# Copies from input to output issued later in the front of a routed MLP kernel

## What is computed

```
xn = rms_w * (x * rsqrt(mean(x * x) + 1e-6))
gate = xn @ wg_W + wg_b + (cond @ gg_W + gg_b)
gate_w = softmax(gate);  topk_w, topk_i = top_k(gate_w, 2)
h1 = relu(x @ W1[e] + b1[e])      # 256 -> 512
h2 = relu(h1 @ W2[e] + b2[e])     # 512 -> 512
out_e = h2 @ W3[e] + b3[e]        # 512 -> 256
return x + sum over the two chosen e of weight * out_e
```

## Time and profile before

| what | before |
|---|---|
| median of 3 runs | 495.13 us (492.8 to 496.7) |
| the profiled execution's own time | 491.41 us |
| its span, first to last instruction | 489.7 us |
| PE busy | 436.9 us (89%) |
| DVE, ACT, POOL busy | 312.3, 291.6, 296.7 us |
| moved by DMA | 44.74 MB |
| on SyncE's queue of it (q1) | 26.26 MB |
| mean granted TensorE clock | 0.953 |

### The profile page before, as it was taken

How to read it: one execution, slowest core, us unless ns; L and a number is a source line. 1 busy time by engine, 2 the same in 40 slices (tenths; PEclk the granted TensorE clock), 3 DMA queues, 4 the chain that set the end, 5 groups by cost and what they waited for, 6 DMA issues and landing times.

```text
span 489.7 us, 13456 instructions
## 1 busy us (share of the span) xinstructions
PE 436.9 (89%) x4330; PEld 390.8 (80%) x4331; DVE 312.3 (64%) x553; ACT 291.6 (60%) x607; POOL 296.7 (61%) x446
## 2 busy tenths in 40 slices
PE   7606979999999999999999999999999999997860
PEld 6406868998888888888988988898899998887850
DVE  4899755756657756756666567555554545867750
ACT  6607725678678678778776764454455455455540
POOL 4420384567777878677777677856655666473331
PEclk9955699999999999999999999999999999999995
DMA  8929234453454543331334322431222233241011
GB/s 297 394 88 368 98 102 168 120 152 58 125 134 127 141 65 111 55 60 27 62 56 126 56 46 40 63 53 35 54 54 43 43 45 53 34 59 22 2 11 12
DMA packets 18771, 44.74 MB, mean 91 GB/s; under 512 B 3964, under 2 KB 13246, under 8 KB 16542
## 3 DMA queue, kind: packets, MB, share of 16 engines
q0 software_dynamic: 13632, 17.71, 22.0%
q1 hardware_dynamic: 5008, 26.26, 14.5%
q10 hardware_dynamic: 77, 0.04, 0.0%
HBM read 35.60 MB, written 13.50 MB: 100 GB/s over the span
## 4 chain that ended last, share of the span: by engine, by line
PE 40%; POOL 19%; issue 13%; DVE 9%; ACT 8%; DMA 4%; POOLq 2%; DVEq 1%; ACTq 0%
PE bank L1156 27%; PE bank L1197 7%; POOL out L556 6%; PE bank L1134 3%; ACT area L705 3%; DMA out<-area,cto 3%; DVE area L958 3%; POOL area L535 2%; POOL bound L480 2%; DVE area L956 2%; ACT w_hi L659 2%; ACT area L715 1%; DVE stage L982 1%; PE bank L1115 1%; POOL cto L530 1%
## 5 line engine op out<-in xcount | busy, mean ns | idle before, releaser
L1156 PE MATMUL bank<-area,w_hi 128*128 128x256 f16 x1536 | 253.7, 273 | 3.4 <-DVE area L958 3.0
L1156 PE MATMUL bank<-area,w_lo 128*128 128x256 f16 x768 | 209.3, 273 | 0.0
L705 ACT ACTIVATE area<-bank,cprm 128x256 f32<-128x256 f32 (+1 forms) x264 | 132.6, 557 | 71.7 <-PE bank L1156 60.8
L1156 PEld LDWEIGHTS bank<-area,w_hi 128*128 x1536 | 149.7, 98 | 22.3 <-issue 5.2
L956 DVE CAST area<-area 128x512 f16<-128x512 f32 (+1 forms) x144 | 65.0, 451 | 133.5 <-ACT area L705 119.9
L556 POOL DMA_INDIRECT out<-area,cto x71 | 117.3, 1652 | 50.4 <-issue 26.1
L958 DVE TENSOR_TENSOR area<-area 128x512 f16<-128x512 f32 (+1 forms) x144 | 99.1, 688 | 5.0
L535 POOL DMA_INDIRECT area<-in_x,cfrom x65 | 68.9, 1061 | 38.9 <-POOL cfrom L530 27.9
L1197 PE MATMUL bank<-w_hi,area 128*128 x512 | 89.1, 273 | 0.9 <-DVE area L958 0.9
L1156 PEld LDWEIGHTS bank<-area,w_lo 128*128 x768 | 75.1, 98 | 8.7
L715 ACT ACTIVATE area<-area,cw 128x256 f32<-128x256 f32 x71 | 32.2, 501 | 76.1 <-DVE area L963 57.4
(11 more groups left out here) (200 smaller groups left out, 478.1 us busy)
## 6 DMA issues: line engine op xcount, KB each, us to landing
stage<-in_weights SPq DMA_DIRECT2D x10, 1024.0 KB, 6.1
area<-in_x SPq DMA_DIRECT2D x8, 512.0 KB, 7.5
out<-in_x SPq DMA_DIRECT2D x8, 512.0 KB, 12.9
w_lo<-in_weights SPq DMA_DIRECT2D x4, 1024.0 KB
w_hi<-in_weights SPq DMA_DIRECT2D x2, 1024.0 KB, 9.0
out<-area,cto POOLq DMA_INDIRECT x71
area<-in_x,cfrom POOLq DMA_INDIRECT x65
prm<-in_b SPq DMA_DIRECT2D x8, 128.0 KB, 11.8
```

What stands on the lines that cost most here:

```text
L705: ins = act.activation(to[:, m * T + u * wide:m * T + (u + 1) * wide], ps_h[layer][b][:, a * T + u * wide:a * T + (u + 1) * wide], ACT.Rel ...
L1156: ins = nc.tensor.matmul(banks[m // 2][:, (m % 2) * T + u * wide:(m % 2) * T + (u + 1) * wide], weight, xp[:, cols], start=(k == 0 and n = ...
```

## The change

The loop that issues the eight copies is taken from its place behind the loads of x. It now stands in the loop over the experts, and runs once, for the third expert (`FRONT` is 2), behind its two chunks of weights and its row of `b3`. Nothing else differs: the same transfers, sizes and semaphores, and POOL's wait on line 599 as it was.

```diff
@@ -388,9 +388,6 @@
                 sp.dma_start(area[:, c * js * H:(c + 1) * js * H],
                              x.rearrange("(p j) h -> p (j h)", p=P)[:, c * js * H:(c + 1) * js * H])\
                   .then_inc(s_x[c], 16)
-            for n in range(OUT_PARTS):
-                rows = slice(n * N // OUT_PARTS, (n + 1) * N // OUT_PARTS)
-                sp.dma_start(out[rows, :], x[rows, :]).then_inc(s_out0, 16)
             sp.wait_ge(s_order, 1)
             labels = []
 
@@ -412,6 +409,9 @@
                     b3_rows(early)
                 if e >= FRONT:
                     b3_rows(e)
+                for n in range(OUT_PARTS if e == FRONT else 0):
+                    rows = slice(n * N // OUT_PARTS, (n + 1) * N // OUT_PARTS)
+                    sp.dma_start(out[rows, :], x[rows, :]).then_inc(s_out0, 16)
 
 
         @block.gpsimd
```

## The result

| | before | after |
|---|---|---|
| median | 495.33 us (490.85 to 498.54, 20 runs) | 498.26 us (494.74 to 501.57, 20 runs) |
| ratio to before, 95% interval | | 1.0068 (1.0042 to 1.0094) |
| profiled execution, its own time | 491.41 us | 498.44 us |
| span | 489.7 us | 496.7 us |
| mean granted clock | 0.953 | 0.948 |

The time lies in the range of the forecast, but "no change" does not hold: the kernel is slower by about 3 us. Single executions of the two kernels overlap, but the interval leaves out 1; the forecast had taken anything within 1% for something that can't be told from no change, and with 20 executions of each kernel 0.7% can be. Each ratio in this document is the recorded one, over executions in the fast state alone and of the same session, and can differ by up to 0.3% from the plain quotient of the medians (1.0059 here).

A forecast was written before the change was run, and what follows sets the result against it. PE's own work was taken to bound 75 to 415 us, and POOL's chain to the gathers the release of tile 0. Five terms of 0 left the median of 495.1 us at 495 us, range 491.5 to 500.

The forecast's parts named there:

- Taking the copies from 13.5 to 25 us: Front, beside x's loads: removing the copies there gains 0, at most the 1.1 us that ACT once waited for x.
- Issuing: SyncE's queue: the eight issues move behind the third expert's b3 and delay nothing, with 26 us of cover; cost 0.
- Moving the bytes: DMA engines from 52.4 us: the copies take 11.3 us, to 63.7 us, filling an 11.0 us hole; cost 0.
- The gathers: Tile 0's gathers at about 63.4 us: 0.3 us overlap with the copies' tail, cost 0; slow end +2.5 us.
- PE's gap above 4 us: Sign of being wrong: PE's idle gap at 63.4 us ahead of tile 0, expected at 2.8 us, exceeds 4 us.
- a low clock between 60 and 100 us: Sign of being wrong: PE's clock is low in that stretch, where full clock was expected behind the gap.
- the second wait of POOL: Sign of being wrong: POOL's wait behind the maximum over partitions, expected at 9.4 to 9.6 us, exceeds 10.5 us.
- The two long waits of POOL: POOL's 9.57 and 9.42 us waits around the maximum over partitions: +0.15 us at most, counted 0; far end +11.3 us.
- The estimate that was made from the Trainium skill's figure: From approximately 6 us for a fresh GpSimd routine's first call: POOL's second long wait would grow by 1.2 us.
- POOL's wait for the copies: Line 599, ending before the copy at 72.52 us: copies through at 63.7 us leave 8.8 us; cost 0.
- The slower rival: PE's gap at 63.4 us: copies delay tile 0 and PE's clock falls, 506 us or 515 us; chance 0.13.

The follow-up runs named there:

- no_copies: The kernel before without the eight copies and without POOL's wait for them, leaving x out of the output: 493.0 us, ratio 0.9983.
- behind_second: The changed kernel with the copies one expert earlier, behind the second expert's weights: 496.06 us, ratio 1.0072.
- warm_after: The changed kernel with 200 in place of 96 unread matmuls of PE ahead of tile 0: 495.01 us, ratio 1.0039.
- small_packets: The changed kernel with each copy written as 128 pieces of 4 KB in place of 16 of 32 KB; profiled packets stayed 32 KB: 497.0 us, ratio 1.0067.
- pad_after: The changed kernel with 40 one-column memsets added to POOL's program where POOL stands idle: 494.47 us, ratio 0.9993.
- six_late: The changed kernel with two of the eight copies back behind the loads of x and six behind the third expert's weights: 493.9 us, ratio 1.0004.
- extra_pad: The changed kernel with 40 memsets added to POOL's program and four more 512 KB copies queued behind its eight: 499.9 us, ratio 1.0129.
- warm_before: The kernel before with 136 in place of 96 unread matmuls of PE ahead of tile 0: 492.18 us, ratio 0.9984.

## Why the prediction was wrong, by its own steps

*Taking the copies from 13.5 to 25 us* was counted at 0 and was 0: no_copies gives 0.9983, with 1 in its interval, so the kernel before had nothing measurable to gain there.

*Issuing* was right. SyncE's queue issues the copies right behind the third b3, and chunk 6 still goes out only when the gather of tile 1 has landed:

```profile
40.33 5.08 SPq L414 DMA_DIRECT2D out<-in_x  x8
75.68 0.87 SPq L405 DMA_DIRECT2D stage<-in_weights  x2
```

*Moving the bytes* was right in place and order: the copies run from the end of the weights. They take 12.8 us and not 11.3 us, inside the 11.3 to 13.6 us that the forecast allowed; it had read their length off slices that count a packet where it starts, and in the kernel before, too, they take 13.1 us from the first start (13.43 us) to the last end (26.48 us). What failed is the conclusion that they "fill a hole". In that hole the engines carried 24 KB of instructions, 8 KB of them in the row at 58 us on which the chain came to depend. The forecast read the 5 and 2 GB/s of the earlier trace rows as emptiness. A sum of small bytes is not a small dependence.

*The gathers* were counted at 0, with the right question (do they meet the copies' tail) and the wrong transfer. Their data was not late. The step that failed is this one together with the list that it belongs to: it names the gathers as the only transfers that could meet the copies, and **has no term for the fetch of POOL's own instructions**. Measured, that term is 2.9 us of wait in the profile of the changed kernel, and 1.5 to 2.4 us more than the usual 0.57 us in those of behind_second, warm_after and small_packets. The forecast gave the second gather a slack of 2.4 us, and in pad_after the gathers did meet the copies' tail and landed on time. The fetch has only 1 us. Two of the forecast's own signs of being wrong came, PE's gap above 4 us (7.2) and a low clock between 60 and 100 us; the second wait of POOL, at 9.1 us, did not.

*The two long waits of POOL* were counted at 0, which stands: together they are 18.99 us before, 19.63 after, 18.6 in pad_after with the copies beside the second, and 19.0 in no_copies. Their sum varies by up to 2.7 us from profile to profile for a reason that these runs don't give. The estimate that was made from the Trainium skill's figure (GPSIMD Engine Reference, section Instruction dispatch) can't be told from that.

*POOL's wait for the copies* cost nothing, as said: it is behind the gathers, at about 76 us, when the copies had been through for 10 us.

*The slower rival* had the right place, PE's gap, and the right second half: with the longer gap came the low clock. It had three things wrong. The first is the cause of the delay. The second is the point from which it decides, a gap of 4.4 us: the clock fell at or right behind gaps of 2.0 to 4.2 us in seven of the profiles. The third is the price: 18 us at half speed, taken from the one stretch of the front in which the clock had come back only at its end. It came back after 6.8 us here, so that the clock's part is about 1.4 us and not 9. With 2.9 + 1.4 = 4.3 us by the profile of the changed kernel, and 2.2 + 1.4 = 3.6 us with the mean wait of the four profiles named above, the sum lies inside what the interval of the ratio allows (2.1 to 4.7 us).

Shown by runs: that the place of POOL's instructions decides, that the copies as such cost nothing measurable in either place, that six of the eight can move for nothing measurable. Argued and not tried: that the packet at 65.16 us is POOL's and not another engine's. It is the only one of its kind in the stretch, it left the stretch when POOL's program was moved, and POOL resumes 2.1 to 2.8 us behind it in each profile with the wait. What smaller packets would do is not tried either, since small_packets did not make them.

## What to carry to other kernels

Before moving a large transfer into a quiet stretch of the DMA engines, look at the stretch in steps of a microsecond for lone packets of the instruction queues, and ask which engine will need them and when. A long wait of an engine "for nothing that the profile shows", right behind bulk transfers, may be its program that is late. An engine that stands idle early can take in its next block then: here 40 empty instructions at an idle place brought back the 3 us that the change had lost, and brought nothing in the kernel before. And of two stretches that would both hide a transfer, the one that does not end just where the next block of instructions or a gather is due is the safer; that is inferred from these runs.

## What the runs showed of the hardware

- A newcomer to DMA engines that are busy with another queue is late. The fetch of instructions was late by 2.4 to 4.7 us with some 4 to 12 us of transfers still queued, copies in 32 KB packets or weights in 8 KB packets, and by 0.5 us with some 2 us queued (six_late). The gathers in extra_pad landed 4.8 us late. The fetch waited neither for one packet of the copies (1.2 to 2.1 us) nor for the whole queue. What sets the amount, and whether the size of the packets matters, stays open.
- An 8 KB block of instructions, taken to be POOL's, starts 3.0 to 3.3 us ahead of the first gather in this kernel when the engines are free. When it is late, the gather is issued 2.1 to 2.8 us behind its start.
- PE's clock fell at or right behind its gap before the work of tile 0 in eleven of the fourteen profiles: for 3.4 us in four (gaps of 2.0 to 4.2 us), for 6.8 us in five (3.6 to 7.2 us) and for 10.2 us in two (7.8 and 9.1 us). It held in the profile before with a gap of 2.8 us, and in warm_before and warm_after, in which unread matmuls shorten the gap to 1.2 us or fill it.
